# Splitting softmax maxima by truncation, with the instruction order laid out anew, in a two-layer decoder kernel

## The reference, cut to what matters

```
x = LN(x + gated linear recurrence(x))
x = LN(x + windowed cross attention(x, context))      # 16 heads of 16, windows of 128
x = LN(x + quantised feed-forward(x))                 # 256 -> 1024 -> 256, GELU
x = LN(x + attention with a position bias(x))         # 16 heads, full 512 x 512
x = LN(x + masked cross attention(x, context))        # softmax times a group weight
x = LN(x + latent causal attention and a mixture of 8 experts(x))
```

## Time and profile before

| | |
|---|---|
| median of three runs | 1494.46 us (1493.71 to 1494.97) |
| profiled execution, span from first to last instruction | 1493.0 us |
| TensorE clock granted, mean | 0.969 of 2.4 GHz |
| PE busy | 1369.8 us (92%) |
| DVE busy | 1085.1 us (73%) |
| ACT busy | 795.1 us (53%) |
| POOL busy | 156.6 us (10%) |

### The profile page before, as it was taken

One profiled execution on the slowest core, in us unless ns is written; L12 is line 12 of the kernel. 1 busy time (PEld: TensorE's weight loads), 2 busy tenths in 40 slices (PEclk: granted clock), 3 DMA queues, 4 the chain that ended last, 5 costly groups with the idle time before them and its releaser, 6 DMA issues. The chain is left out here.

```text
span 1493.0 us, 29555 instructions
## 1 busy us (share of the span) xinstructions
PE 1369.8 (92%) x9483; PEld 763.5 (51%) x9519; DVE 1085.1 (73%) x2623; ACT 795.1 (53%) x1507; POOL 156.6 (10%) x185
## 2 busy tenths in 40 slices
PE   6878989999999999999999999999999989889990
PEld 3556566664454544443353343343545445578990
DVE  5786744457664777789999999998868877563325
ACT  5375755536647666665455465555666545323332
POOL 1101011100100100001010000000000003224223
PEclk8799999999999999999999999999999989999996
DMA  6223323301402542434343333122222231676754
GB/s 230 79 68 102 104 48 86 86 26 27 127 23 80 163 122 52 137 94 121 104 143 98 93 123 86 51 65 53 62 53 56 52 105 57 206 292 194 213 182 179
DMA packets 124482, 158.32 MB, mean 106 GB/s; under 512 B 31372, under 2 KB 103820, under 8 KB 122348
## 3 DMA queue, kind: packets, MB, share of 16 engines
q1 hardware_dynamic: 120930, 147.06, 33.9%
q0 software_dynamic: 3408, 9.38, 1.7%
HBM read 66.38 MB, written 29.44 MB: 64 GB/s over the span
## 5 line engine op out<-in xcount | busy, mean ns | idle before, releaser
L1668 ACT ACTIVATE prob<-ps 128x512 f32<-128x512 f32 (+3 forms) x832 | 404.0, 550 | 202.8 <-PE ps L1441 108.1
L1960 DVE TENSOR_REDUCE mx<-ps 128x1 f32<-128x512 f32 (+3 forms) x512 | 281.3, 585 | 80.3 <-PE ps L1409 42.4
L1441 PE MATMUL ps<-of_expert 99*128 99x512 bf16 (+4 forms) x768 | 252.4, 357 | 8.2 <-DMA of_expert<-mrow 3.3
L1441 PEld LDWEIGHTS ps<-of_expert 99*128 99x128 bf16 (+1 forms) x768 | 73.1, 98 | 95.5 <-ACT prob L1668 35.7
L1476 PE MATMUL ps<-prob,va 128*32 128x512 f32 (+3 forms) x1024 | 117.0, 530 | 0.2
L1407 PE MATMUL ps<-of_expert 120*128 120x512 bf16 x256 | 92.0, 380 | 3.6 <-DVE mx L1960 0.4
L1401 PE MATMUL ps<-of_expert 96*128 96x512 bf16 x256 | 86.7, 381 | 6.2 <-DVE mx L1956 5.3
L1956 DVE CUSTOM_DVE_ANT_0 ps<-ps,room_a 128x512 f32<-128x512 f32 x128 | 86.1, 710 | 5.5 <-PE ps L1401 5.2
L1956 DVE CUSTOM_DVE_ANT_0 ps<-ps,room_b 128x512 f32<-128x512 f32 x128 | 85.9, 708 | 1.7 <-PE ps L1401 1.4
L1398 PE MATMUL ps<-of_expert 96*128 96x128 bf16 (+3 forms) x256 | 72.4, 306 | 9.0 <-DVE mx L1960 7.3
L1658 ACT ACTIVATE mrow<-ps 12x512 bf16<-12x512 bf16 x64 | 37.2, 581 | 77.3 <-PE ps L1423 77.2
(11 more groups left out here) (251 smaller groups left out, 2550.4 us busy)
## 6 DMA issues: line engine op xcount, KB each, us to landing
of_expert<-parts SPq DMA_DIRECT2D x384, 128.0 KB, 2.4
sorted<-zeros SPq DMA_DIRECT2D x27, 650.0 KB, 7.7
room_a<-in_w SPq DMA_DIRECT2D x30, 512.0 KB, 4.1
otc<-oraw SPq DMA_DIRECT2D x256, 32.0 KB, 2.0
room_b<-in_w SPq DMA_DIRECT2D x15, 512.0 KB, 4.2
ct<-in_c SPq DMA_DIRECT2D x8, 512.0 KB, 3.8
of_expert<-in_w SPq DMA_DIRECT2D x8, 512.0 KB, 8.2
wa<-in_attention SPq DMA_DIRECT2D x4, 768.0 KB, 5.0
```

Of the source, the lines that this page charges most:

```text
L1441: i = pe.matmul(dst[:, lo:S], ks[0:rows, h, t], qs[0:rows, h, lo:S], start=(a != MASKED), stop=(a != CAUSAL and not fixed))
L1668: act.activation(prob[:, quad % PROBS, n, lo:S], key_bank(*st)[:, lo:S], ACT.Exp).then_inc(s_exp, 1)
L1960: i = dve.tensor_reduce(mx[:, slot, s, n:n + 1], src[:, 0:width], AX.X, ALU.max)
```

## The change

1. `mp` (bf16 parts) and `mr` (rest) are gone. `mx` holds three float32 numbers per maximum. Part 0 is the maximum itself, part 1 is part 0 less its own upper half read as bf16 (truncation), part 2 is part 1 less its own upper half. So P has two dependent instructions, both `tensor_tensor`, in place of four.
2. The transposes of M read the upper halves of the three float32 numbers as their bf16 weights, with a step of 4 bytes in place of 2. The parts are no longer negated by P; the copy to `mrow` negates with `scale=-1.0`.
3. The wait for M four groups earlier moves from P to the first S reduction of a group on DVE.
4. The plan: all step times, `HOP` (per engine now), `LANDING` and the table `LAG` have new values, P is planned at 0.4 for 0.8, the place of the moved wait is planned, and the token sort SX is planned after the zero fills ZF. So `ORDER` and the places of the dummy matmuls are new for every engine's stream.

```diff
-    mm = 0.91
+    mm = 0.865
...
-        dve = 0.6 if a in (WINDOW, ALIBI) else 0.67 if a == MASKED else 0.07 + 0.133 * (s + 1)
+        dve = 0.6 if a in (WINDOW, ALIBI) else 0.65 if a == MASKED else 0.07 + 0.133 * (s + 1)
...
-        return [("DVE", 0.8, [(("S", u, g, quads(u) - 1, J - 1), "DVE")] + ([(("M", i // G, i % G), "PE")] if i >= 0 else []))]
+        return [("DVE", 0.4, [(("S", u, g, quads(u) - 1, J - 1), "DVE")])]
...
-        return [("PE", 0.25, room + [(("P", u, g), "DVE")]), ("ACT", 0.6, [(("M", i // G, i % G), "SP")] if i >= 0 else []),
-                ("SP", 0.6, [], 0.1)]
+        return [("PE", 0.26, room + [(("P", u, g), "DVE")]), ("ACT", 0.47, [(("M", i // G, i % G), "SP")] if i >= 0 else []),
+                ("SP", 0.8, [], 0.1)]
...
-        pe, act = 0.23, 0.56
+        pe, act = 0.218, 0.49
...
-        return [("DVE", 1.15, [(("T", u, g, s, 2 * h + 1), "ACT")] + more)]
+        return [("DVE", 1.09, [(("T", u, g, s, 2 * h + 1), "ACT")] + more)]
...
-        return [("POOL", 2.54, [(("RB", k), "DVE")] + front, 1.3)]
+        return [("POOL", 2.54, [(("RB", k), "DVE"), (("ZF", FILLS - 1), "SP")] + front, 1.3)]
...
-HOP = 0.15
-LANDING = 1.9
+HOP = {"PE": 0.31, "ACT": 0.14, "DVE": 0.13, "POOL": 0.15, "SP": 0.1}
+LANDING = 1.4
...
-LAG = {"IN": -3.7, "CA": 26.5, ("CA", 1): 25.9, "FS": 13.8, "OP": -5.3, ("OP", 0): 1.6, ("OP", 1): -4.0, ("OP", 3): 2.1, "M":
+LAG = {"IN": 1.4, "EI": 11.3, ("EI", 0): -11.3, ("EI", 1): 36.9, ("EI", 2): 0.6, "EA": -0.4, "CA": 186.7, ("CA", 0): 1.0,
...
-        mx = sb("mx", [P, MAXIMA, NT, J])
-        mr = sb("mr", [P, NT, J])
-        mp = sb("mp", [P, MAXIMA, NT, 3, J], BF16)
+        mx = sb("mx", [P, MAXIMA, NT, 3, J])
...
+        def upper(z):
+
+            return z.bitcast(BF16)[:, 1::2]
+
+        def upper_of_max(slot, i):
+
+            whole = mx[:, slot, :, :, :].rearrange("p q i j -> p (q i j)").bitcast(BF16)
+            return whole.rearrange("p (q i j h) -> p q i j h", q=NT, i=3, j=J)[:, :, i, :, 1]
...
-                            i = pe.transpose(rows_out[0:3 * J, q * P:(q + 1) * P], mp[:, slot, q, :, :].rearrange("p i j -> p (i j)"), identb)
+                            i = pe.transpose(rows_out[0:3 * J, q * P:(q + 1) * P], upper(mx[:, slot, q, :, :].rearrange("p i j -> p (i j)")), identb)
...
-                    act.activation(mrow[g % 2][:, :], key_bank(*st)[0:3 * J, :].bitcast(BF16)[:, 0:S], ACT.Copy).then_inc(s_mc, 1)
+                    act.activation(mrow[g % 2][:, :], key_bank(*st)[0:3 * J, :].bitcast(BF16)[:, 0:S], ACT.Copy, scale=-1.0).then_inc(s_mc, 1)
...
+                    if s == 0 and n == 0 and G * u + g >= MAXIMA:
+                        before = G * u + g - MAXIMA
+                        dve.wait_ge(s_mt, nth("M", before // G, before % G))
...
-                    if G * u + g >= MAXIMA:
-                        before = G * u + g - MAXIMA
-                        dve.wait_ge(s_mt, nth("M", before // G, before % G))
-                    dve.tensor_scalar(p3[:, :, 0, :], m, -1.0, None, ALU.mult).then_inc(s_v, mine.one())
-                    dve.wait_ge(s_v, mine.count)
-                    dve.scalar_tensor_tensor(mr[:, :, :], m, -1.0, p3[:, :, 0, :], ALU.mult, ALU.subtract).then_inc(s_v, mine.one())
-                    dve.wait_ge(s_v, mine.count)
-                    dve.tensor_copy(p3[:, :, 1, :], mr[:, :, :]).then_inc(s_v, mine.one())
-                    dve.wait_ge(s_v, mine.count)
-                    dve.tensor_tensor(p3[:, :, 2, :], mr[:, :, :], p3[:, :, 1, :], ALU.subtract).then_inc(s_mp, 1)
+                    dve.tensor_tensor(parts_of_max[1], parts_of_max[0], upper_of_max(slot, 0), ALU.subtract).then_inc(s_v, mine.one())
+                    dve.wait_ge(s_v, mine.count)
+                    dve.tensor_tensor(parts_of_max[2], parts_of_max[1], upper_of_max(slot, 1), ALU.subtract).then_inc(s_mp, 1)
```

More of the change, by code:

```diff
@@ L361, in parts_of @@
     if kind == "LP":
-        return [("PE", 2 * mm, side + loaded("lora")), ("ACT", 0.6, [])]
+        return [("PE", 2 * mm, side + loaded("lora")), ("ACT", 0.49, [])]
     if kind == "QM":
@@ L399, in parts_of @@
         b, = rest
-        return [("PE", 2 * mm, side + [(("SC", b), "DVE")] + loaded("pack")), ("ACT", 1.2, [])]
+        return [("PE", 0.9, side + [(("SC", b), "DVE")] + loaded("pack")), ("ACT", 0.97, [])]
     if kind == "LS":
@@ L424, in parts_of @@
             xt = [(("UP", b - 1, NF - 1), "PE")] if b else [(("QZ", 1, 1), "DVE")]
-        return [("PE", 0.6, side + [(src, "DVE" if src[0] == "RZ" else "ACT")]), ("ACT", 0.6, xt)]
+        return [("PE", 0.45, side + [(src, "DVE" if src[0] == "RZ" else "ACT")]), ("ACT", 0.49, xt)]
     if kind == "XB":
@@ L439, in parts_of @@
         out = [("PE", 2 * mm, side + [(("GE", b, j // 2), "ACT")] + more)]
-        return out + ([("DVE", 0.65, [(("XB", NB + b, 0), "POOL")])] if j == 3 else [])
+        return out + ([("DVE", 0.6, [(("XB", NB + b, 0), "POOL")])] if j == 3 else [])
     if kind == "LT":
         u, = rest
-        return [("PE", 2 * mm, side + [(("TR", u, 1, 1), "ACT")]), ("ACT", 0.6, [(("VP", u - 1, 1), "PE")])]
+        return [("PE", 2 * mm, side + [(("TR", u, 1, 1), "ACT")]), ("ACT", 0.49, [(("VP", u - 1, 1), "PE")])]
     if kind == "QK":
@@ L451, in parts_of @@
         room = [(("OP", u - 1, piece_of(u - 1, g), o), "SP") for g in (2 * c, 2 * c + 1)] if u else []
-        return [("PE", (1 if o and a == CAUSAL else 2) * mm, side + more), ("ACT", 0.7, room), ("DVE", 0.65, [])]
+        return [("PE", (1 if o and a == CAUSAL else 2) * mm, side + more), ("ACT", 0.58, room), ("DVE", 0.66, [])]
     if kind == "SL":
         u, o = rest
-        return [("ACT", 1.05, [(("QK", u, o, 1), "DVE")]), ("DVE", 1.15, [])]
+        return [("ACT", 0.95, [(("QK", u, o, 1), "DVE")]), ("DVE", 1.12, [])]
     if kind == "VP":
@@ L460, in parts_of @@
         room = [(("V", u - 2, G - 1, quads(u - 2) - 1), "PE")] if u > 1 else []
-        return [("PE", (1 if a == CAUSAL else 2) * mm, side + more), ("DVE", 0.7, room)]
+        return [("PE", (1 if a == CAUSAL else 2) * mm, side + more), ("DVE", 0.66, room)]
     if kind == "OP":
@@ L541, in parts_of @@
             more += [(("C", i // G, i % G), "ACT")]
-        return [("PE", 0.15 + {WINDOW: mm, ALIBI: mm, MASKED: 2 * mm, CAUSAL: mm * (NT - s) / NT}[a], more)]
+        return [("PE", 0.165 + {WINDOW: 0.8, ALIBI: mm, MASKED: 2 * mm, CAUSAL: mm * (NT - s) / NT}[a], more)]
     if kind == "C":
@@ L546, in parts_of @@
         more = [(("C", i // G, i % G), "SP"), (("R", i // G, i % G), "DVE")] if i >= 0 else []
[L547 removed]
+        return [("ACT", 0.49, [(("V", u, g, quads(u) - 1), "PE")] + more),
                 ("SP", 3.05, [(("OU", u - 1, 1), "PE")] if u else [], 0.6)]
@@ L561, in parts_of @@
         load = [(("WO", a), "SP")] if a else loaded("wo")
-        return [("PE", 2 * mm, side + [(("N", u, 1), "DVE")] + load), ("DVE", 1.3 if a == CAUSAL else 0.65, more)]
+        return [("PE", 2 * mm, side + [(("N", u, 1), "DVE")] + load), ("DVE", 1.2 if a == CAUSAL else 0.6, more)]
     if kind == "HT":
         b, c = rest
-        return [("PE", 0.6, side + [(("RZ", b, 6), "DVE")]), ("ACT", 0.6, [(("RO", b - 1), "PE")] if b else [])]
+        return [("PE", 0.45, side + [(("RZ", b, 6), "DVE")]), ("ACT", 0.49, [(("RO", b - 1), "PE")] if b else [])]
     if kind == "RO":
         b, = rest
-        return [("PE", 2.1, side + [(("HT", b, 1), "ACT")]), ("DVE", 0.25, [])]
+        return [("PE", 1.8, side + [(("HT", b, 1), "ACT")]), ("DVE", 0.25, [])]
     if kind == "RA":
@@ L580, in parts_of @@
         k, = rest
-        return [("PE", 0.3, side + [(("RK", b), "DVE") for b in BATCHES[k]] + [(("RC",), "SP")]), ("DVE", 7.0, [])]
+        return [("PE", 0.1, side + [(("RK", b), "DVE") for b in BATCHES[k]] + [(("RC",), "SP")]), ("DVE", 8.3, [])]
     if kind == "SX":
@@ L689, in plan @@
             free[engine] = at
-            at += HOP
+            at += HOP[engine]
             if moved:
```

45 lines of the change are left out of this document (22 added, 23 removed), and 29 rows, old and new, of the table LAG.

## The result

| | before | after |
|---|---|---|
| median | 1494.61 us (1493.71 to 1494.97, 4 runs) | 1477.09 us (1473.79 to 1478.70, 4 runs) |
| profiled execution, span | 1493.0 us | 1472.0 us |
| ratio after / before | | 0.9875, 95% interval 0.9861 to 0.9889 |

The medians differ by 17.5 us where 14.5 was forecast (1480.0, range 1465 to 1497). The profiled execution of after is its fastest one, 1473.79 us with 1.8 us around the span, so the difference of the two traces, 21.0 us, is 3.5 us more than that of the medians.

What follows compares the result with a forecast made beforehand. DVE was taken to bound MASKED, PE ALIBI, and order and chain latencies WINDOW and CAUSAL. 1493.0 - 6.6 - 2.9 - 0 - 5 = 1478.5 us, plus 1.46 to the median: 1480.0 us, range 1465 to 1497.

Steps and rivals of the forecast that it cites:

- The sum: Whole kernel: 1493.0 - 6.6 - 2.9 - 0 - 5 = 1478.5 us, plus 1.46 from span to median: 1480.0; chance 0.40.
- MASKED is bound by DVE, 6.6 us: MASKED, 16 groups: DVE sets the pace, so 0.41 us saved per group leaves the stage, 6.6 us.
- The test that I named for it: MASKED: stretch between first and last reduction of L1956 6 to 8 us shorter, DVE still above 95% busy.
- The other 48 groups, 2.9 us: Outside MASKED: 0.41 us counts only at 7 waits for the split or its DMA, 2.9 us; bounds 0 and 19.7.
- Transposes, copy, moved wait: 0: Weight loads with 4-byte step, the copy with scale -1, and DVE's wait moved to the first reduction: each 0 us.
- The new order, 5 us: All streams permuted: 5 us gained of 89.7 us idle PE and dummies outside MASKED and ALIBI; bounds 22 gain, 15 loss.
- Its own sign: Order right if idle PE plus dummies in start up, WINDOW, CAUSAL and experts fall below 89.7 us.
- fewer stretches at half clock: Seven PE stretches at half clock, 32.8 us, cost about 16 us; with none left up to 16 us won.
- Too early T: Rival, WINDOW and CAUSAL: T planned too close behind the mrow DMA; 20 more PE waits give 1503 us; chance 0.18.
- The clock: Rival: the new order has four more half-clock stretches of 6.7 us, losing 13.4 us: 1493 us; chance 0.09.
- Only the split: Rival: the new order is worth nothing in either direction, 1494.46 - 9.5 = 1485 us; chance 0.20.
- The order wins more, 22 us: Rival: the order wins a quarter of the 89.7 us idle PE and dummies, 1463 us; chance 0.13.

Runs made afterwards that it cites:

- the pad: Four more dependent instructions in P on the new split in the old order: in MASKED only 1.0061, in the other stages only 0.9996 of before.
- the split alone: Kernel before with only the new two-instruction split; order, step times and dummies of before: ratio 0.9948 to before, 7.8 us.
- the new order up to MASKED: New split; new order up to the first masked score, remaining steps in the old order: ratio 0.9889 to before, median 1480.2 us.
- the runs without dummies: Dummy matmuls removed from the kernel after and from the new split in the old order: ratios 0.9989 and 1.0022 to before.
- the new order from MASKED on: New split; old order up to the first masked score, remaining steps in the new order: ratio 0.9942 to before.
- the order alone: Kernel after with the old split of four instructions put back; order, step times and dummies of after: ratio 0.9927 to before, 10.9 us.

## Why the prediction was right, and where it was not

**The sum.** The number lies in the forecast's own range of 1474 to 1484 us, and that is partly luck: the split was put 1.7 us too high (9.5 for 7.8) and the order 5.9 us too low (5 for 10.9), two misses that partly cancel. The prediction also set a mark that was passed: it called itself wrong as a whole "if the order moves more than 10 us on its own". The order moved 10.9 us, with an error of 3.4 that reaches to both sides of the mark. By its own test, then, the account of the order failed, while that of MASKED stood. The 1.46 us between span and median came from two different executions; the runs show 1.8 us around a span, which changes the forecast by 0.3.

*MASKED is bound by DVE, 6.6 us.* Right in kind: with the order held fixed the split shortens the stretch by 5.1 and 4.1 us, and the pad lengthens it by 0.93 us per us added in it. A little too large, because the saving is 0.38 us a group and only 15 of the 16 P lie ahead of the last masked reduction: 15 x 0.38 = 5.7 us. The test that I named for it was wrong: "the stretch between the first and the last reduction is 6 to 8 us shorter" fails in the kernel after, where the new order moved E into it; with the order held fixed 5.1 us is still a little under its 6.

*The other 48 groups, 2.9 us.* The pad gives 3.6 us (error 1.6), if taking steps away is worth what adding them costs. The direct pair of traces shows 0.8 us (5.9 us of span less the 5.1 of MASKED), and the medians 2.7 with an error of 2.8. So it is shown that these groups count for far less than 48 x 0.41 us, but not that they give 2.9. The whole split: 9.5 forecast, 7.8 measured (error 2.8).

*Transposes, copy, moved wait: 0.* Right for the load, 88 ns. The prediction called the 174 ns of L1976 "every occurrence"; the row has a longest one of 177, which changes nothing. In the list of PE's waits after, the split is late for 0.6 us in all where it was 5.2. The moved wait shows nowhere among DVE's waits.

*The new order, 5 us.* This is the mis-sized term: it measured 10.9 us (error 3.4). The step that failed is "what can be won is idle PE and dummies, and only outside MASKED and ALIBI". Its own sign went the wrong way: idle PE plus dummies, counted as it counted them, were to fall below 89.7 us and are 15.3 + 42.9 + 30.9 + 11.4 = 100.5 us after, and yet the kernel is faster. Idle PE fell by 8.4 us and dummies took more than its place. The place was wrong too. Start up and WINDOW in the new order, with the put off steps done ahead of ALIBI, win nothing; with ALIBI in the new order as well 8.8 us are won. I took 350.0 of 360 us busy for a bound and left the 10 us of idle PE out, but it is there that room was found: idle PE in ALIBI goes from 10.3 us with the split alone to 4.4 with the new order up to MASKED, and the stretch takes in work that stood ahead of it. That the gain needs the order of ALIBI is shown; that it comes through this side work is read from the counts.

I also held that fewer stretches at half clock could win up to 16 us and gave them no share of the forecast. Behind 72 us and ahead of the last 37 they sum to 32.8 us before and 19.2 us after, six of them (the first and the sum, trace of after):

```profile
86.70:89.90 3.20, 3.20 (x27) 3.14 (x28) 3.10 (x4) 2.48 (x5) 0.86 (x1) 0.50 0.04 6
...
sum 19.20, PE 19.02 PEld 14.38 DVE 12.99 ACT 7.88 POOL 4.26; mean PE 3.17 PEld 2.40 DVE 2.17 ACT 1.31 POOL 0.71
```

What the 13.6 us less are worth is not shown. Half of them, 6.8 us, is the most, if all work in them takes twice as long; at the 0.22 us that the runs without dummies give it is 3 us. Other runs speak against the clock as the carrier of the order's gain. The mean clock over all executions is 0.9700 for the split alone and 0.9707 with the new order up to MASKED, which is 8.8 us faster; it is 0.9730 with the new order from MASKED on, which is 0.9 us faster.

*The rivals.* Too early T: the DMA of `mrow` was late 7 times for 9.8 us after, where it was 6 times for 7.0, far from the 12 more that would decide. The rows after:

```profile
PE ps L1450 <- DMA of_expert<-mrow: 5.1, 3, 2.3
...
PE ps L1443 <- DMA of_expert<-mrow: 4.7, 4, 3.1
```

The clock went the other way. Only the split: refuted by the order alone at 0.9927. The order wins more, 22 us: this had the direction, but the 10.9 us lie nearer to the 5 that were forecast.

## What to carry to other kernels

When an order and an instruction change together, compare no stretch between two marks until the work inside it is counted: here four instructions of 1.2 us hid a true gain. To learn what a step is worth, hold the order and pad the step in one stage at a time: the same added instructions cost nearly their full time where DVE is 96% full and about a fifth of it elsewhere. Adding steps tells what more would cost, and is only a hint at what fewer would save: here 6.6 us against nothing ahead of MASKED. A busy share of PE of 97% is no proof that a new order can win nothing there. A planner's step times and its fitted table belong together: new step times with the old table cost 7%.

## What the runs showed of the hardware that was not expected

A short DVE instruction on SBUF can be held up while GpSimd works on SBUF too. One of the 64 first steps of the split took 1.58 us for 0.175, inside a GpSimd `tensor_tensor` of 2.0 us (trace of after, start, us):

```profile
136.27 2.00 POOL L1794 TENSOR_TENSOR x<-x,pack 128x1024 f32<-128x1024 f32 x1 [10.20 <-PE ps L1260]
136.71 1.58 DVE L1979 TENSOR_TENSOR mx<-mx 128x16 f32<-128x16 f32 x1
138.33 0.17 DVE L1981 TENSOR_TENSOR mx<-mx 128x16 f32<-128x16 f32 x1
```

It ends at 138.29 us, the GpSimd instruction at 138.27. It is not the new form that does it: with the old split in the new order the first of the four steps, which has one tensor operand, meets the same once (durations min/median/max in ns, and the place):

```profile
L1972 DVE TENSOR_SCALAR mp<-mx x64: 168/175/1582, 60.0 to 1268.1; 128x16 bf16<-128x16 f32 x64
...
140.61 2.00 POOL L1787 TENSOR_TENSOR x<-x,pack 128x1024 f32<-128x1024 f32 x1 [10.62 <-PE ps L1253]
...
141.05 1.58 DVE L1972 TENSOR_SCALAR mp<-mx 128x16 bf16<-128x16 f32 x1
```

The Trainium skill (VectorE: DVE Perf Modes, section "Two Vector instructions with no wait between them") says that the engine's second SBUF read interface is shared with GpSimd. The rows fit that; no run here tests it. With the new split in the old order none of the 64 first steps took more than 216 ns, so it depends on where the order puts them.
